# ScalarE in place of VectorE scales the attention's exponentials by the inverse of their row sums, behind the next unit's exponentials

## The reference

```python
q, k, v = x @ W_Q[h].T, x @ W_K[h].T, x @ W_V[h].T
scores = where(causal, -1e9, q @ k.T / sqrt(128))
pattern = softmax(scores)
out = sum over h of (pattern @ v) @ W_O[h].T
x = layernorm(x + out)
```

## Time and profile before

| | |
|---|---|
| median of 3 runs | 1584.14 us (1581.84 to 1587.19) |
| the profiled execution | 1599.27 us, its span 1597.1 us |
| attention, eight groups | about 25 to 608 us of the span |
| TensorE busy over the span | 1498.2 us (94%) |
| VectorE | 1116.0 us (70%) |
| ScalarE | 745.6 us (47%) |
| GpSimd | 503.4 us (32%) |
| mean granted TensorE clock | 0.985 |

### The profile page before, as it was taken

The page is one execution under the profiler, slowest core; times in us unless marked ns, Lnnn a source line. Parts: engine busy times, 40 slices in busy tenths (PEclk is TensorE's granted clock), DMA queues, the critical chain, the costliest instruction groups (busy, mean ns, idle before and its releaser), DMA issues.

```text
span 1597.1 us, 29158 instructions
## 1 busy us (share of the span) xinstructions
PE 1498.2 (94%) x9433; PEld 1309.8 (82%) x9433; DVE 1116.0 (70%) x3031; ACT 745.6 (47%) x1968; POOL 503.4 (32%) x355
## 2 busy tenths in 40 slices
PE   7999999999999988999999999999998599999897
PEld 5988888888989877887888888888787488988776
DVE  5878788787878776655558678867968447532687
ACT  5666666675666543333523353244323444454221
POOL 3323222222323102432346325644671212000550
PEclk9999999999999999999999999999999699999999
DMA  7564645464655104665676557656664489798774
GB/s 267 201 222 169 241 173 210 151 240 159 231 197 184 67 1 147 189 191 182 206 225 211 166 173 220 195 186 201 204 205 133 142 279 299 247 288 269 248 249 143
DMA packets 129737, 315.87 MB, mean 198 GB/s; under 512 B 15968, under 2 KB 39216, under 8 KB 128608
## 3 DMA queue, kind: packets, MB, share of 16 engines
q1 hardware_dynamic: 125024, 301.95, 57.7%
q0 software_dynamic: 4608, 12.59, 2.3%
HBM read 225.35 MB, written 88.60 MB: 197 GB/s over the span
## 4 chain that ended last, share of the span: by engine, by line
PE 49%; issue 21%; DVE 13%; POOL 10%; ACT 4%; DMA 1%; SPq 0%; DVEq 0%; ACTq 0%; POOLq 0%
PE psum L512 43%; POOL act_sb L837 5%; POOL mix L855 3%; PE psum L1733 2%; POOL xs L867 1%; DVE s_sb L1315 1%; PE psum L1744 1%; ACT p_sb L969 1%; PE psum L1723 1%; PE psum L1969 1%; ACT kT_hi L928 1%; PE psum L1938 1%; DVE s_sb L1313 1%; DVE kT_lo L1197 1%; DVE pT_lo L1330 1%
## 5 line engine op out<-in xcount | busy, mean ns | idle before, releaser
L512 PE MATMUL psum<-xT_hi,gu_w 128*128 128x512 f32 x1088 | 373.8, 403 | 16.5 <-DVE act_sb L1464 9.3
L837 POOL TENSOR_TENSOR act_sb<-act_sb,comb 128x512 f32<-128x512 f32 x96 | 159.4, 1660 | 374.9 <-DVE act_sb L1464 374.9
L512 PEld LDWEIGHTS psum<-xT_hi,gu_w 128*128 128x128 f32 x1088 | 206.2, 190 | 70.7 <-issue 15.2
L1010 ACT ACTIVATE gated<-psum 128x512 f32<-128x512 f32 (+1 forms) x138 | 82.4, 597 | 388.9 <-PE psum L512 364.3
L1464 DVE TENSOR_TENSOR act_sb<-psum,gated 128x512 f32<-128x512 f32 (+1 forms) x138 | 95.0, 688 | 184.4 <-PE psum L512 161.6
L512 PE MATMUL psum<-xT_lo,gu_w 128*128 128x512 f32 x544 | 216.3, 398 | 0.4 <-issue 0.4
L791 POOL TENSOR_TENSOR split_stage<-raw_stage,split_stage 128x768 fp32r<-128x768 f32 x56 | 102.9, 1838 | 352.3 <-ACT split_stage L918 352.3
L512 PEld LDWEIGHTS psum<-d_w,act_hi 128*128 128x128 f32 (+1 forms) x1104 | 150.2, 189 | 13.3 <-issue 1.5
L512 PE MATMUL psum<-d_w,act_hi 128*128 128x256 f32 (+1 forms) x1104 | 154.7, 283 | 0.0
L967 ACT ACTIVATE p_sb<-s_sb,neg_max 128x128 f32<-128x128 f32 x128 | 51.5, 403 | 172.0 <-DVE neg_max L1315 172.0
L512 PEld LDWEIGHTS psum<-xT_lo,gu_w 128*128 128x128 f32 x544 | 103.2, 190 | 19.1
(11 more groups left out here) (257 smaller groups left out, 4025.5 us busy)
## 6 DMA issues: line engine op xcount, KB each, us to landing
gu_w<-w_split SPq DMA_DIRECT2D x138, 512.0 KB
w_split<-split_stage SPq DMA_DIRECT2D x56, 768.0 KB, 4.0
d_w<-w_split SPq DMA_DIRECT2D x138, 256.0 KB
bw<-l_w SPq DMA_DIRECT2D x63, 496.0 KB, 3.5
xs<-zeros SPq DMA_DIRECT2D x21, 1280.0 KB, 7.5
raw_stage<-w_all SPq DMA_DIRECT2D x56, 384.0 KB, 4.5
decay_all<-decay_dram SPq DMA_DIRECT2D x32, 384.0 KB, 4.8
in_w<-w_split SPq DMA_DIRECT2D x40, 256.0 KB
```

Of the source, the lines that this page charges most:

```text
L512: last = nc.tensor.matmul(out_ap, w, m, start=start and n == 0, stop=stop and n == len(pairs) - 1, **kw)
L837: pool.tensor_tensor(act_sb[:, s % 2, :], act_sb[:, s % 2, :], comb[:, comb_block(s) % 2, :], ALU.mult).then_inc(comb_done, 1)
L1010: act.activation(gated[to, s % 2, :], psum[0:to.stop - to.start, G_BANK, :], ACT.Silu).then_inc(gated_ready, 1)
```

## The change

VectorE keeps the reciprocal. Its two multiplications go, and with them its wait for its own reciprocal. ScalarE does them as ACTIVATE with the function Identity and the inverse as a per-partition scale, in place, in the same step as before, behind the exponentials of the next unit and ahead of the copies of the step. ScalarE now waits for `r_ready`; `p_scaled` is signalled by it. The computation is the same.

```diff
@@ ScalarE, group, in step i behind the exponentials of unit i
+                    if 0 <= i - 1 < UNITS:
+                        u = i - 1
+                        act.wait_ge(r_ready, g * UNITS + u + 1)
+                        act.activation(p_sb[:, u % 3, 0:P], p_sb[:, u % 3, 0:P], ACT.Identity, scale=row_inv[:, u % 3, 0:1])
+                        act.activation(p_sb[:, u % 3, P:3 * P], p_sb[:, u % 3, P:3 * P], ACT.Identity, scale=row_inv[:, u % 3, 1:2]).then_inc(p_scaled, 1)
@@ VectorE, group
                         u = i - 1
                         dve.wait_ge(p_ready, g * UNITS + u + 1)
                         dve.reciprocal(row_inv[:, u % 3, :], row_sum[:, u % 3, :]).then_inc(r_ready, 1)
-                        dve.wait_ge(r_ready, g * UNITS + u + 1)
-                        dve.tensor_scalar(p_sb[:, u % 3, 0:P], p_sb[:, u % 3, 0:P], row_inv[:, u % 3, 0:1], None, ALU.mult)
-                        dve.tensor_scalar(p_sb[:, u % 3, P:3 * P], p_sb[:, u % 3, P:3 * P], row_inv[:, u % 3, 1:2], None,
-                                          ALU.mult).then_inc(p_scaled, 1)
```

## The result

The changed kernel takes 1652.5 us (median of 4 runs, 1651.4 to 1655.3), against 1585.7 us for the kernel before in the same comparison. The ratio is 1.0415 (95% interval 1.0395 to 1.0435): 67 us slower. The forecast was 1646 us.

A forecast was written before the change was run, and what follows sets the result against it. TensorE paces the attention, with a ScalarE-VectorE loop at the same pace. A round goes from 72.8 us by 7.7 to 80.5; eight rounds add 62 us, giving 1646 us on the median; range +45 to +75 us, chance 0.66.

The forecast's parts named there:

- The loop: Attention: mask, exponentials, copy, subtractions, next mask form a chain of ScalarE and VectorE; 14 steps each grow by 0.69 us.
- TensorE's stall in step 12: Attention round: TensorE would stall 2.0 us at the transposes of step 12, waiting for pT_lo.
- The price of the pair: ScalarE's two added ACTIVATEs a unit cost 0.69 us, taken from rows of exponentials nearest in form.
- The lower bound of 0.42: The pair's cost in us if the scale costs nothing over plain copies, from the spacing of pT_last and pT_hi.
- The place, not the load: The pair, behind the exponentials and ahead of the copies, is in the loop; ScalarE's 1.35 us idle lies ahead of the exponentials.
- The gain: Removing VectorE's scaling ends GpSimd's holds in steps 1, 5, 9, 11 and 13: 2.15 us less a round.
- The last round: Attention's eighth round, without next projection but with layernorm work on VectorE: pair again in series, 7.7 us longer.
- The cheap pair: Rival: the pair costs 0.42 us as plain copies do, +4 us a round, 1616 us; chance 0.17.
- no change: Rival: the pair falls into ScalarE's 1.35 us of idle time a unit, 1584 us; chance 0.04.
- The faster one: Rival: VectorE's hold is what TensorE waits for; earlier masks remove 27 us of stalls, 1557 us; chance 0.08.
- The clock rival: Rival: clock drops after TensorE's stalls, up to 1.7 us a round, 1660 us; more than +75 us had 0.05.
- table load: Rival: loads at each change between Exp and Identity, 2 x 1.28 us a unit, over 300 us; more than +75 had 0.05.

The follow-up runs named there:

- e7_xadd: Changed kernel, pair in its place, with VectorE's addition of a finished output to x moved behind the next mask and reciprocal; ratio 1.0250, a round of 77.65 us.
- e2_imm: Changed kernel with the pair in its place as plain Copy without the per-partition scale, leaving out the division; ratio 1.0251, a round of 77.68 us.
- e3_both: Kernel before, VectorE still scaling, plus a same-shaped ScalarE pair behind the exponentials that writes a spare tile; ratio 1.0418, a round of 80.60 us.
- e1_end: Changed kernel with the pair moved behind all copies of ScalarE's step, ahead of the expert weights' split; ratio 0.9961, a round of 71.67 us.
- e4_none: Kernel before with the scaling removed from VectorE and put on no engine; the reciprocal signals p_scaled; ratio 0.9933, a round of 71.33 us.
- e6_first: Changed kernel with the pair moved behind the copy of the step's first projection job; one execution, a round of 77.07 us.
- e9_xadd_only: Kernel before, VectorE still scaling, with only the addition into x moved behind the next mask and reciprocal; ratio 1.0009, a round of 73.17 us.
- e10_both_end: Kernel before, VectorE still scaling, plus a same-shaped pair at the end of ScalarE's step that writes spare tiles; one execution, a round of 74.20 us.

## Why the prediction was right

**The loop.** Right. For the four steps from mask 5 to mask 9 the prediction's terms give 17.14 + 4 x 0.69 - 0.31 - 0.17 - 0.49 = 18.93 us (it said about 19), and they took 18.96. Mask 15 was forecast 6.5 us late and is 6.5 late; the transposes of step 16 at 71.3, found at 71.4; what follows in the round was forecast 0.5 longer and is 0.6; the round was forecast at 80.5 and is 80.66. TensorE's stall in step 12 was forecast at 2.0 us and is 1.76. e7_xadd shows the loop apart from the pair.

**The price of the pair.** Right: 0.69, from exponentials of the same shape and an exponential with a per-partition scale; the rows after have 0.388 and 0.495 us, spaced 0.30 and 0.39. The lower bound of 0.42 was taken from copies out of PSUM and was too low for this pair: in e2_imm plain copies in SBUF are spaced 0.20 and 0.31, 0.51 together. Identity with the scale lasts 0.09 us longer than Copy, at either width; as the function and the operand were changed together, no run says which of the two it is. The page "ScalarE: Activation LUTs" of the Trainium skill (What ACT_TABLE_LOAD costs) has 93 ns for each per-partition operand. The runs, with 94 and 93 ns, agree with it.

**The place, not the load.** Right, and by now shown by four places of the same pair.

**The gain.** Here a step failed in its meaning, though not in the sum. "2.15 us a round, and this is the gain of the change": GpSimd's holds do leave the loop, but not because VectorE's scaling is removed. e3_both keeps the scaling and its holds and has the same round. The pair makes each copy 0.69 us later, and a hold that reached 0.31 to 0.70 past the copy then ends before or with it. So such a step grows by 0.69 less the lateness that it had, whether VectorE still scales or not: the term was right to subtract and wrongly named. That e3_both and the changed kernel agree to 0.1 us shows it. By itself the removal is worth 1.47 us a round, not 2.15; TensorE, which has 69.8 us to do in that round of 71.3, leaves little more to gain.

**The last round.** Mis-sized: 7.7 was taken over from the others, and it grew by 9.0 us (70.5 to 79.5, first scores to last transposes). GpSimd has no split to do there, and in the trace of before only one scaling of this group lasts over 0.7 us (0.89), so there was next to nothing of the 2.15 to subtract. Without it the sum would have given 9.8; the other 0.8 was not followed. The windows of the last group, before and after (GpSimd's busy time is the last of the five):

```profile
532.28:602.80 70.52, 62.93 (x440) 56.76 (x439) 53.20 (x204) 36.54 (x136) 2.69 (x8) 0.98 0.01 1
```

```profile
587.57:667.10 79.53, 65.01 (x440) 56.90 (x438) 43.66 (x172) 47.11 (x168) 2.58 (x8) 0.98 0.00 1
```

With seven rounds at 7.88 instead of 7.7 this gives 55.2 + 9.0 = 64 us where the sum had 62.

**The rivals.** The cheap pair (1616) and no change are out, by the measured price and the measured time. The faster one, 1557 us, named a real effect, VectorE's relief, but with the pair in the loop it is worth nothing (e3_both), and without it e1_end and e4_none price it at 1.1 to 1.5 us a round, 9 to 12 us in all and not 27. The 0.2 us that it puts to each stall beside the idle time is of the right size: the round after has nine more stalls of over 0.1 us and 2.55 us more of busy time, 0.28 each. The clock rival came once and not once a round: in the seventh round the granted clock was 0.76 over 7 us (as 3.4 us at the lower level, 1.2 GHz, would give), and the other full rounds were at 1.00. It fell 1.2 us after the stall of step 12 had ended, and it cost nothing: this round is 80.68 us long like the others. In e6_first it fell three times, each time within 2 us after that stall, and its rounds are all 77.06 to 77.11 us. While the loop sets the pace, TensorE has the time to spare. No table load came with Identity: the pair follows the exponential without a gap, and ScalarE has no ACT_TABLE_LOAD between 2 and 667 us of the trace.

```profile
560.00:567.00 7.00, 5.82 (x31) 5.36 (x32) 3.98 (x17) 5.22 (x19) 2.55 (x2) 0.76 0.40 121
```

**What was left.** The ratio's interval is 63 to 69 us, so the 64 us of the attention lie within it; the 3 us up to the measured 67 were not followed.

## What to carry to other kernels

Before work is moved to a less busy engine, find the chain that passes between the two and see on which side of its link the idle time lies: here ScalarE was idle for 1.35 us a unit, ahead of the exponentials, and work of 0.69 us a unit put behind them, 11.0 us a round, made the round 7.9 us longer, while the same work at the end of the step cost 0.3 (e1_end against e4_none). Work that runs beside the loop on one engine (VectorE's scaling beside the exponentials) is worth little to remove, however busy that engine is: VectorE's busy time of a round fell by 15.7 us in e4_none, and the round by 1.5. When a chain of two engines and TensorE run at the same pace, take things out of the chain together: the addition alone gave nothing, the scaling alone 0.4%, both 1.0%.

## What the runs showed of the hardware

SBUF to SBUF, Identity with a per-partition scale takes 0.094 us more at 128 columns and 0.093 more at 256 than Copy without one (0.388 and 0.495, against 0.294 and 0.402), so the difference doesn't grow with the columns.

In the attention VectorE's tensor_scalar in SBUF is held while GpSimd's tensor_tensor runs (0.29 us become up to 1.55). The other wide forms there read PSUM, and none was held: in the changed kernel, with the same GpSimd work, no instruction of VectorE in a round lasts over 0.70 us. Behind the attention there are others in SBUF that are long beside GpSimd's work, such as the subtraction for act_lo, which takes 0.68 us in the median and up to 4.96. Which of its ops meets GpSimd's decides what a hold costs, and moves with every change of order (e9_xadd_only, e10_both_end).
